# Attention scores in three PSUM banks, one head per exponential, and a fourth bank for the maxima

## The reference

```
x = x + attn0(layernorm(x));  x = x + ffn0(layernorm(x))
x = x + attn1(layernorm(x));  x = x + ffn1(layernorm(x))
attn: 16 heads of dimension 16; scores q.k / 4 (layer 0: plus a per-head slope times the key's position)
      causal mask; softmax over keys; times v; heads side by side; times Wo
ffn:  down(silu(gate(x)) * up(x))
```

## Time and profile before

| | us |
|---|---|
| median of 3 runs | 454.28 (452.84 to 456.42) |
| the profiled execution, its time | 454.21 |
| its span in the trace | 452.5 |
| PE busy | 413.6 (91%) |
| DVE busy | 302.1 (67%) |
| ACT busy | 236.0 (52%) |
| POOL busy | 157.5 (35%) |

### The profile page before, as it was taken

One profiled execution on the slowest core, in us unless ns is written; L12 is line 12 of the kernel. 1 busy time (PEld: TensorE's weight loads), 2 busy tenths in 40 slices (PEclk: granted clock), 3 DMA queues, 4 the chain that ended last, 5 costly groups with the idle time before them and its releaser, 6 DMA issues.

```text
span 452.5 us, 14388 instructions
## 1 busy us (share of the span) xinstructions
PE 413.6 (91%) x6264; PEld 233.6 (52%) x6264; DVE 302.1 (67%) x608; ACT 236.0 (52%) x380; POOL 157.5 (35%) x228
## 2 busy tenths in 40 slices
PE   0799989999999979999999998898999999798997
PEld 0347754454555338434466455644545553374476
DVE  1475799999997119412234577999999971197893
ACT  1374645677677872311100552455777778725950
POOL 4177023202202221295951100234362564211870
PEclk9999999999999999999999999999999999998999
DMA  8999550000000000202000378500000000000002
GB/s 176 153 256 237 124 139 4 4 4 3 5 1 6 4 6 1 71 0 70 0 1 0 100 194 196 144 5 4 3 4 4 4 4 4 2 0 1 1 20 74
DMA packets 23922, 22.95 MB, mean 51 GB/s; under 512 B 5194, under 2 KB 23114, under 8 KB 23850
## 3 DMA queue, kind: packets, MB, share of 16 engines
q1 hardware_dynamic: 22132, 19.02, 18.2%
q0 software_dynamic: 608, 2.50, 2.0%
q10 hardware_dynamic: 1120, 0.53, 0.5%
HBM read 8.27 MB, written 1.05 MB: 21 GB/s over the span
## 4 chain that ended last, share of the span: by engine, by line
PE 73%; DVE 15%; ACT 5%; DMA 3%; issue 2%; POOL 1%; SPq 0%; ACTq 0%; DVEq 0%
PE ps L678 11%; PE ps L658 11%; PE ps L636 10%; PE ps L761 9%; DVE mx L1031 9%; PE ps L800 7%; PE ps L776 5%; PE ps L766 5%; ACT prob L923 4%; PE ps L784 3%; PE ps L575 3%; DMA x<-in_L_attn_x 2%; PE ps L584 2%; PE ps L644 2%; DVE stats L996 1%
## 5 line engine op out<-in xcount | busy, mean ns | idle before, releaser
L1031 DVE TENSOR_REDUCE mx<-ps 128x1 f32<-128x512 f32 (+3 forms) x304 | 182.1, 654 | 25.8 <-PE ps L644 22.5
L923 ACT ACTIVATE prob<-ps 128x1024 f32<-128x1024 f32 (+1 forms) x192 | 145.6, 812 | 70.5 <-PE ps L658 69.9
L636 PE MATMUL ps<-kS,qS 99*32 99x512 bf16 (+19 forms) x1536 | 112.9, 319 | 4.4 <-DVE mx L1031 3.4
L490 POOL TENSOR_SCALAR_AFFINE_SELECT prob<-prob 128x256 f32<-128x256 f32 x128 | 52.0, 412 | 166.4 <-ACT prob L923 165.1
L658 PE MATMUL ps<-qS,kS 101*32 101x512 bf16 (+7 forms) x1536 | 96.3, 327 | 4.9 <-ACT prob L923 3.5
L678 PE MATMUL ps<-prob,v 128*32 128x512 f32 (+3 forms) x768 | 80.2, 489 | 2.1 <-POOL prob L490 1.4
L636 PEld LDWEIGHTS ps<-kS,qS 99*32 99x32 bf16 (+1 forms) x1536 | 43.0, 95 | 51.8 <-DVE mx L1031 29.4
L658 PEld LDWEIGHTS ps<-qS,kS 101*32 101x32 bf16 (+1 forms) x1536 | 35.3, 96 | 32.1 <-ACT prob L923 16.8
L641 PE MATMUL ps<-mask_q,identb 128*32 128x32 bf16 (+1 forms) x1024 | 51.1, 185 | 0.0
L644 PE MATMUL ps<-mask_q,identb 128*32 128x96 bf16 (+1 forms) x512 | 45.5, 197 | 0.0
L761 PE MATMUL ps<-xnT,gu0T 128*128 128x512 f32 (+1 forms) x96 | 42.2, 596 | 0.7 <-ACT xnT L839 0.7
(11 more groups left out here) (127 smaller groups left out, 521.8 us busy)
## 6 DMA issues: line engine op xcount, KB each, us to landing
qS<-parts SPq DMA_DIRECT2D x24, 128.0 KB, 3.2
kS<-parts SPq DMA_DIRECT2D x24, 128.0 KB, 3.9
qS<-prob SPq DMA_DIRECT2D x12, 128.0 KB, 4.9
kS<-prob SPq DMA_DIRECT2D x12, 128.0 KB, 5.0
qS<-xn SPq DMA_DIRECT2D x12, 128.0 KB
kS<-xn SPq DMA_DIRECT2D x12, 128.0 KB, 2.5
x<-in_L_attn_x SPq DMA_DIRECT2D x2, 512.0 KB, 7.7
out<-x SPq DMA_DIRECT2D x8, 128.0 KB, 1.7
```

The lines of the kernel that those rows point to most:

```text
L490: nc.gpsimd.affine_select(out=square, in_=square, compare_op=ALU.is_ge, fill=0.0, base=0, pattern=[[0, 2], [1, P]], channel_multiplier=-1) ...
L636: mmi = nc.tensor.matmul(span[r:r + STRIP, 0:seen], qS[0:K_MAX[L], c, g * G + h, qt * P + r:qt * P + r + STRIP], kS[0:K_MAX[L], g * G + h, ...
L923: nc.scalar.activation(prob[:, n % 3, 2 * pair:2 * pair + 2, off:CH], ps[:, 2 * (m % 2):2 * (m % 2) + 2, off:CH], ACT.Exp, scale=SCALE).th ...
L1031: ins = nc.vector.tensor_reduce(mx[:, slot, qt, heads[0]:heads[-1] + 1, part], src, AX_X, ALU.max)
```

## The change

The scores' banks become three, 0 to 2, used by single heads in rotation: head m of all heads (four per step) goes into bank m mod 3, and PE writes it after ACT has finished head m-3. PE signals after each head, ACT's exponential works on one head (128 x up to 512) instead of two, and signals after each, so there are 384 such instructions instead of 192. POOL and pv wait for the same heads as before, counted one by one. Bank 3 joins banks 4 to 6 for the maxima once the first exponentials of the layer are in the list (before that, side jobs use it); a function gives each item the least recently used bank and the count to wait for. The order of PE's entries is unchanged.

```
-M_BANKS = 3
+S_BANKS = 3
+def max_banks():
+    banks, last, wait = [], {}, []
+    late = False
+    for e in ORDER:
+        late = late or e == ("exp", 0, 0)
+        if e[0] in ("max", "turn"):
+            free = range(S_BANKS, 7) if late else range(S_BANKS + 1, 7)
+            bank = min(free, key=lambda b: last.get(b, -1))
+            wait.append(last.get(bank, -1) + 1)
+            last[bank] = len(banks)
+            banks.append(bank)
+    return banks, wait
...
 max_scores:
-                bank = ps[:, 4 + n % M_BANKS]
+                bank = ps[:, MAX_BANK[n % N_MAX]]
...
 exp_scores:
-                n = 2 * (L * N_STEP + s) + pair
-                if n >= 2:
-                    pe.wait_ge(s_free, n - 1)
                 for i in range(2):
+                    n = 4 * (L * N_STEP + s) + 2 * pair + i
+                    if n >= S_BANKS:
+                        pe.wait_ge(s_free, n - S_BANKS + 1)
                     h = g * G + 2 * pair + i
-                    bank = ps[:, 2 * (n % 2) + i]
+                    bank = ps[:, n % S_BANKS]
...
-                mmi.then_inc(s_full, 1)
+                    mmi.then_inc(s_full, 1)
...
 attention, for an item and for a turn:
-                            pe.wait_ge(m_free, m_n - M_BANKS + 1)
+                            pe.wait_ge(m_free, L * N_MAX + MAX_BANK_WAIT[m_n % N_MAX])
...
 ACT:
-                    for pair in range(G // 2):
-                        m = 2 * n + pair
+                    for h in range(G):
+                        m = 4 * n + h
                         act.wait_ge(s_full, m + 1)
-                        nc.scalar.activation(prob[:, n % 3, 2 * pair:2 * pair + 2, off:CH],
-                                             ps[:, 2 * (m % 2):2 * (m % 2) + 2, off:CH], ACT.Exp, scale=SCALE).then_inc(s_free, 1)
+                        nc.scalar.activation(prob[:, n % 3, h, off:CH], ps[:, m % S_BANKS, off:CH], ACT.Exp, scale=SCALE).then_inc(s_free, 1)
```

More of the change, by code:

```diff
@@ L207 @@
 LAST_STEP = {cg: max(s for s, x in enumerate(STEPS) if x[0] == cg) for cg in range(N_CG)}
+def max_banks():
[10 more added lines that the diff above has]
+    return banks, wait
+MAX_BANK, MAX_BANK_WAIT = max_banks()
 def step_span(s):
@@ L487, in cut_triangles @@
                     for pair in range(G // 2):
-                        pool.wait_ge(s_free, 2 * n + pair + 1)
+                        pool.wait_ge(s_free, 4 * n + 2 * pair + 2)
                         square = prob[:, n % 3, 2 * pair:2 * pair + 2, off:off + P]
@@ L672, in times_v @@
                 else:
-                    pe.wait_ge(s_free, 2 * (n + 1))
+                    pe.wait_ge(s_free, 4 * (n + 1))
                 if kt == 0 and L * N_CG + cg >= 1:
@@ L695, in attention @@
                                 ready.add(n)
-                        if m_n - L * N_MAX >= M_BANKS or L:
-                            pe.wait_ge(m_free, m_n - M_BANKS + 1)
+                        if m_n and (L or MAX_BANK_WAIT[m_n]):
+                            pe.wait_ge(m_free, L * N_MAX + MAX_BANK_WAIT[m_n % N_MAX])
                         max_scores(L, m_n, cg, item)
@@ L704, in attention @@
                         cg = entry[1]
-                        pe.wait_ge(m_free, m_n - M_BANKS + 1)
+                        pe.wait_ge(m_free, L * N_MAX + MAX_BANK_WAIT[m_n % N_MAX])
                         pe.wait_ge(mneg_done, L * N_CG + cg + 1)
-                        nc.tensor.transpose(ps[0:2 * G * TPC, 4 + m_n % M_BANKS, 0:P // 2].bitcast(BF16),
+                        nc.tensor.transpose(ps[0:2 * G * TPC, MAX_BANK[m_n % N_MAX], 0:P // 2].bitcast(BF16),
                                             mneg[:, cg % 2].rearrange("p s h t -> p (s h t)"), identb[:]).then_inc(m_full, 1)
@@ L722, in out_projection @@
                 pe.wait_ge(o_taken, (L + 1) * N_CG)
-                pe.wait_ge(s_free, 2 * (L + 1) * N_STEP)
+                pe.wait_ge(s_free, 4 * (L + 1) * N_STEP)
                 for t in range(NT + 2):
@@ L1029, in attention @@
                         dve.wait_ge(m_full, m_n + 1)
-                        src = ps[:, 4 + m_n % M_BANKS, 0:len(heads) * keys].rearrange("p (h k) -> p h k", h=len(heads))
+                        src = ps[:, MAX_BANK[m_n % N_MAX], 0:len(heads) * keys].rearrange("p (h k) -> p h k", h=len(heads))
                         ins = nc.vector.tensor_reduce(mx[:, slot, qt, heads[0]:heads[-1] + 1, part], src, AX_X, ALU.max)
@@ L1043, in attention @@
                             dve.wait_ge(m_stacked[n % 2], 16 * (n // 2))
-                        nc.vector.tensor_copy(mT[:, entry[1] % 2], ps[0:2 * G * TPC, 4 + m_n % M_BANKS, 0:P // 2].bitcast(BF16)).then_inc(mT_done, 1)
+                        nc.vector.tensor_copy(mT[:, entry[1] % 2], ps[0:2 * G * TPC, MAX_BANK[m_n % N_MAX], 0:P // 2].bitcast(BF16)).then_inc(mT_done, 1)
                         dve.wait_ge(mT_done, n + 1)
```

## The result

The changed kernel takes 470.06 us (median of 4 runs, 466.43 to 471.46) against 454.74 us of the kernel before on the same chip: a ratio of 1.0347, with a 95% interval of 1.0302 to 1.0392. Forecast were 474.5 us, 465 to 484, slower. The profiled execution is the shortest of the four, 466.43 us with a span of 464.7.

What follows compares the result with a forecast made beforehand. PE bounds steps 12 to 35, DVE steps 0 to 11, ACT and PE alternate in 36 to 47. Terms 12.7 + 2.6 + 1.0 + 4.0 = 20.3 on 454.2 gave 474.5 us, range 465 to 484.

Steps and rivals of the forecast that it cites:

- The halt before the fourth head: Each full step: PE waits for ACT's first exponential, 1.165 us against 0.87 of work, halting 0.30 us.
- The sum over a group: Groups of 8 steps in steps 12 to 35: halts sum to 2.41 us, 14.5 in six groups.
- What is absorbed: Steps 12 to 35: fourth maxima bank removes short halts, 0.3 us per group, 1.8 in six, leaving +12.7.
- The fourth maxima bank: PE runs four items ahead of DVE; buys nothing in steps 4 to 11, only short halts in 12 to 35.
- +2.6: Steps 4 to 11: halts not covered by PE's idle time add 1.3 us a layer, +2.6 us.
- +1.0: Steps 0 to 3: 1.45 us of halts against 2.16 idle, most covered; +1.0 us for both layers.
- Steps 36 to 47: End of each layer: full steps at 2.24 us, group 6 +1.3, group 7 +0.4 and +0.3; +4.0 us for two layers.
- ACT's instructions: 384 one-head exponentials, 0.165 us fixed, 595 ns for 512, stride 0.49; no throughput cost in steps 12 to 35.
- One sign: Changed profile: ACT busy about 25 to 30 us more by latency, its idle time still charged to PE.
- Nothing that counts: Rival: halts fall into waits PE has anyway; 450 to 459 us, some 456; chance 0.08.
- faster: Rival: ACT's earlier start and the fourth bank remove PE's idle time in steps 0 to 11; 448 us; chance 0.05.
- The full fixed cost on the path: Rival: each of 192 extra ACT instructions puts its 0.165 us on the path, 32 us, 486; chance 0.07.

Runs made afterwards that it cites:

- the dose: Changed kernel with two score banks instead of three, maxima in four banks as before; 498.31 us, ratio 1.0989.
- the split alone: Kernel before with each exponential of a pair issued as two instructions, one per head, only the second signalling; 461.13 us, ratio 1.0130.

## Why the prediction was right, point by point

*The halt before the fourth head.* Forecast 1.165 us from the first head to the fourth for 512 columns, 1.00, 0.84 and 0.68 for 384, 256 and 128. In the trace of groups 4 to 6 they start 1.15 us apart for 512 columns where nothing else is ahead of them on ACT, and 0.99 to 1.01, 0.83 to 0.89 and 0.67 to 0.70 for the others. The parts hold too: in step 20 the four matmuls take 0.39, ACT starts 0.11 later, its first exponential lasts 0.60, and PE starts 0.05 after it. Two banks give the dose, four take it away. This step is shown.

*The sum over a group.* For group 4 the forecast halts were 0.30, 0.47, 0.27, 0.12, 0.37, 0.29, 0.29 and 0.30; read from the trace (third to fourth head, after less before) they are 0.28, 0.47, 0.25, 0.11, 0.23, 0.30, 0.33 and 0.28, together 2.26 instead of 2.41. The fifth was wrong because the item between its pairs is one of two heads, 0.28 us and not 0.14.

*What is absorbed.* This term was mis-sized: I allowed 0.3 us a group, and group 4 went from 18.06 to 19.80 us, +1.74, so 0.52 of the 2.26 are absorbed. And I gave it to the wrong cause: not the fourth bank (the dense steps are the same with three), but short waits that PE had before and that now pass during a halt. In group 4 of the kernel before these are 0.09 us behind the copy of oT, 0.11 for DVE in step 23, 0.14 at the turn in step 25 and 0.18 for POOL at pv in step 27, 0.52 together; these are the steps that lengthen by less than their halt (by 0.09, 0.10, 0.15 and 0.19). Over all six groups the halts come to 13.8 us (forecast 14.5), of which 2.9 are absorbed (allowed 1.8), and that makes 10.9 instead of 12.7.

*The fourth maxima bank.* "Where DVE has no gap this buys nothing" failed: by the traces it buys 0.6 us in step 0 and 0.6 in step 4 of each layer, and 1.8 us in all. With three maxima banks steps 0 to 11 of both layers take 63.2 and 63.4 us in the two traces, 1.2 and 1.4 above the 62.0 of the kernel before, in the direction of the 3.6 forecast; with four they take 61.7 and 61.6. The halts in these steps come to 6.7 us (forecast 8.3), and some four fifths of them are covered even without the bank. So the terms +2.6 and +1.0 are the ones sized most wrong. (The prediction also gives DVE's 18.66 of 18.85 us for steps 0 to 11; these are steps 4 to 11, and in steps 0 to 3 DVE is busy 10.72 of 11.81.)

*Steps 36 to 47.* Forecast +4.0, measured +4.0, in part by luck: per layer group 6 took 1.5 us more instead of 1.3 (15.1 to 16.6) and group 7 0.5 instead of 0.7. Full steps take 2.24 to 2.30 us once in stride (2.24), narrow ones 2.03, 1.60 and 1.20 (2.03, 1.60, 1.18), the second step of group 7 2.89 after 1.64.

*ACT's instructions.* The fixed part was right, 0.165 us (614 and 278 ns for 512 and 128 elements leave 0.166 beside 0.875 ns per element), the stride of 0.49 too (2.06 us for four). The mean of 614 ns is above the 595 forecast, but the exponential that the fourth head waits for starts on an idle ACT and lasts 597; those behind the copy of oT last 660 to 690. That the rate is free where ACT is idle was right where every head signals by itself, as the run with four score banks shows, but the split alone, with one signal a pair, cost 3.8 us; the 1.165 had this inside, since it used 0.595 for one head. One sign did not come: ACT is 13.5 us busier, not 25 to 30, because the profile counts time in which two instructions overlap once (384 of 502 ns would be 193 us, and their busy time is 159.7).

*The rivals.* "Nothing that counts" (456) and "faster" (448) fell with the result itself. The full fixed cost on the path (486) fell with the run of four score banks, which has the 192 instructions more and no difference, and with the split alone, 6.6 us by the medians instead of 32. The kernel with four score banks also has the 192 increments more on PE, 48 of them in each dense stretch, and its dense stretches are 0.20 and 0.14 us longer than before. By the Trainium skill's 26.3 ns per increment (TensorE: Matmul & The Clock Gate, The cost: per-tile semaphore tail) 48 would be an estimated 1.3 us; the traces here don't show that.

*The sum.* The mechanism was right, and the terms together were too large: 20.3 us forecast, 14.6 in the traced stretches, with 3.9 of the difference in steps 0 to 11 and 1.8 in steps 12 to 35. That the forecast of 474.5 lies only 4.4 above the median of 470.06 is partly luck, since 3.1 us of the medians' difference are in no trace. The profiled execution, 466.43, lies inside the range as well.

## What to carry to other kernels

In a ring of k buffers on an in-order engine, add up the way of one buffer (write, drain, start of the reader, read, signal) and compare it with the time that the writer needs for the k-1 others and what stands between them in its program; if the way is longer, the difference is paid each time around when the writer is the bound, less what the writer would have waited anyway (here 10.9 of 13.8 us were paid). Fewer, smaller buffers can be enough in bytes and still too few in time: here three banks of one head hold 1.15 us of latency over 0.87 us of work. When the order can't give the writer more work in between, a move to behind a long instruction helps only if what hangs on the moved piece (here the triangle on POOL) has room to be late.

## What the runs showed that I had not expected

Short halts added to one place took away others elsewhere: a quarter of the halts of a dense group (0.52 of 2.26 us) cost nothing, because PE's own small waits for ACT, DVE and POOL then ran out unseen. And in layer 0's last steps the granted clock fell to the lower level after PE had been busy only 0.36 of the microsecond before, in both profiled executions with three score and three maxima banks and in neither of the two of the changed kernel, though the halts are the same and PE is just as little busy (0.36 and 0.37); it costs 1.3 us there. With two score banks, where PE halts longest, it fell there too, and steps 36 to 47 took 30.5 us in layer 0 against 28.5 in layer 1, where it stayed at 1.00. What decides it I can't say.
